# Holding the second half of the first input loads until half of the first mix is done

## What is computed

```
feature: (512, 200, 64) float32      weight: (200, 64, 64) float32
bilinear = einsum('bie,ied->bid', feature, weight)
out      = einsum('bid,bjd->bij', bilinear, feature)      # (512, 200, 200)
```

## Time and profile before

| what | value |
|---|---|
| median of 3 runs | 310.88 us (308.45 to 311.99) |
| the profiled execution | 306.8 us |
| its span, first to last instruction | 305.0 us |
| mean granted TensorE clock | 0.961 |
| TensorE matmuls busy | 243.2 us (80%) |
| VectorE / ScalarE / GpSimd busy | 50% / 43% / 4% |
| DMA, mean over the span | 368 GB/s |

### The profile page before, as it was taken

One profiled execution on the slowest core, in us unless ns is written; L12 is line 12 of the kernel. 1 busy time (PEld: TensorE's weight loads), 2 busy tenths in 40 slices (PEclk: granted clock), 3 DMA queues, 4 the chain that ended last, 5 costly groups with the idle time before them and its releaser, 6 DMA issues.

```text
span 305.0 us, 14640 instructions
## 1 busy us (share of the span) xinstructions
PE 243.2 (80%) x6800; PEld 210.9 (69%) x6800; DVE 152.8 (50%) x180; ACT 130.1 (43%) x181; POOL 12.5 (4%) x23
## 2 busy tenths in 40 slices
PE   6839849999877586999867785898985774998990
PEld 2437749888776476878866675866885674996970
DVE  0153634556755443537644454634765554775621
ACT  2153515445544324245444243542653451665420
POOL 2004800000000000000000000000000000000000
PEclk9996997999999979899999799999999999999997
DMA  7999997999999999968999999986999999599995
GB/s 219 415 417 357 363 410 302 324 376 373 369 360 416 407 419 420 409 280 354 374 366 408 383 411 417 388 355 248 389 371 391 408 387 417 210 402 381 409 408 218
DMA packets 22172, 112.35 MB, mean 368 GB/s; under 512 B 4320, under 2 KB 4320, under 8 KB 21856
## 3 DMA queue, kind: packets, MB, share of 16 engines
q1 hardware_dynamic: 22112, 111.43, 92.6%
HBM read 29.49 MB, written 81.92 MB: 365 GB/s over the span
## 4 chain that ended last, share of the span: by engine, by line
PE 76%; issue 16%; DMA 2%; SPq 2%; DVE 1%; ACT 1%
PE psum L322 50%; PE psum L285 17%; PE psum L339 8%; DMA w_sb<-w_dram 2%; SPq L166 2%; PE psum L305 1%; DVE tile L355 1%; ACT mixed L376 0%; ACT w_sb L390 0%; SPq L178 0%
## 5 line engine op out<-in xcount | busy, mean ns | idle before, releaser
L322 PE MATMUL psum<-x_sb,mixed 64*64 64x200 f32 x3072 | 163.1, 351 | 14.0 <-issue 12.5
L322 PEld LDWEIGHTS psum<-x_sb,mixed 64*64 64x64 f32 x3072 | 133.3, 139 | 27.9 <-issue 17.9
L355 DVE COPY tile<-psum 128x800 f32<-128x800 f32 x100 | 99.2, 992 | 88.6 <-PE psum L322 79.8
L355 ACT COPY tile<-psum 128x800 f32<-128x800 f32 x100 | 82.4, 826 | 70.2 <-PE psum L322 54.0
L285 PE MATMUL psum<-x_sb,w_sb 64*64 64x64 f32 x3072 | 64.4, 221 | 35.1 <-issue 34.2
L285 PEld LDWEIGHTS psum<-x_sb,w_sb 64*64 64x64 f32 x3072 | 61.7, 134 | 40.5 <-issue 37.7
L376 ACT COPY mixed<-psum 64x512 f32<-64x512 f32 x48 | 27.8, 580 | 43.2 <-PE psum L285 42.6
L376 DVE COPY mixed<-psum 64x512 f32<-64x512 f32 x48 | 33.1, 689 | 16.7 <-PE psum L285 15.5
L378 ACT COPY mixed<-psum 128x512 f32<-128x512 f32 x24 | 14.1, 586 | 36.3 <-PE psum L285 36.2
L378 DVE COPY mixed<-psum 128x512 f32<-128x512 f32 x24 | 16.6, 691 | 22.3 <-PE psum L285 22.2
L339 PE MATMUL psum<-x_sb,tails 128*32 128x200 f32 x512 | 25.0, 342 | 0.1
(11 more groups left out here) (5 smaller groups left out, 1.7 us busy)
## 6 DMA issues: line engine op xcount, KB each, us to landing
out_dram<-tile SPq DMA_DIRECT2D x192, 400.0 KB, 5.6
x_sb<-x_dram SPq DMA_DIRECT2D x64, 400.0 KB, 6.9
out_tail_dram<-tile SPq DMA_DIRECT2D x8, 400.0 KB, 4.2
w_sb<-w_dram SPq DMA_DIRECT2D x1, 1152.0 KB, 15.2
w_sb<-w_dram SPq DMA_DIRECT2D x4, 256.0 KB, 7.3
w_sb<-w_dram SPq DMA_DIRECT2D x1, 1024.0 KB, 13.1
```

Of the source, the lines that this page charges most:

```text
L322: last = nc.tensor.matmul(psum[half_rows(pair), n % BANK_PAIRS * 2 + h, a * FIELDS:(a + 1) * FIELDS], mixed[half_rows(h), (CHUNKS * g + c) ...
L355: copy(tile[:, k % SLOTS, engine], psum[:, bank:bank + 2, 0:2 * FIELDS]).then_inc(copied[engine], 1)
```

## The change

SP now waits, behind W pieces 1 to 3, until TensorE has finished two of the four units of the first mix. Then come part 1's first two loads (its piece 0), W piece 4, part 1's other six loads, and W piece 5. The order of these is changed only in that W piece 4 stands behind two of part 1's loads and not behind all eight. No other engine's program changes.

```
@@ -183,10 +183,16 @@
                 load_part0(sp, 0, n)
             for n in range(1, MIX_UNITS):
                 load_w(n)
-            for n in range(X_LOADS):
+
+
+            sp.wait_ge(unit_ready, MIX_UNITS // 2)
+
+            for n in range(X_STRIPS):
                 load_part1(sp, 0, n)
-            for n in range(MIX_UNITS, len(W_CUTS) - 1):
-                load_w(n)
+            load_w(MIX_UNITS)
+            for n in range(X_STRIPS, X_LOADS):
+                load_part1(sp, 0, n)
+            load_w(MIX_UNITS + 1)
```

## The result

The changed kernel takes 310.39 us in the median of 12 runs (307.5 to 313.09), the kernel before 309.99 us in 12 (308.45 to 311.99). The ratio on record is 1.011, interval 1.0068 to 1.0151: slower by about 1%, where the forecast said 1% faster. That ratio is taken over fast runs alone, and the runs listed here don't reproduce it: the means of the 12 and 12 are 310.4 and 310.3 us. Two more timings gave ratios of 1.0068 (1.001 to 1.0126) and 1.0059 (0.9997 to 1.012). Over all timings the mean of 36 runs of the changed kernel is 311.0 us (standard error 0.5), that of 110 runs of before 309.6 us (0.2): 1.4 us slower, give or take 0.5. Timing by timing the means differ by 0.1, 1.4 and 1.7 us. So the change brings no gain, and it costs about 1 us, which is not far outside the noise. A single profile can't show so little at its end: spans of the same code scatter by several us.

What follows compares the result with a forecast made beforehand. TensorE, busy 80% of 305.0 us, loses some 50 us to stalls, read as late instruction pages. Of a 4.4 us lead 2.95 us stay: 306.8 to 303.85 us profiled, 310.88 to 307.9 us median; range 305.0 to 312.5 us.

Steps and rivals of the forecast that it cites:

- What the stalls are: TensorE's stalls without a semaphore: ends of 256-instruction pages where the next page was not there; first one 3.59 us.
- the rival built on it: First mix: the 3.59 us stall is no late page, so it stays; 310.9 us, chance 0.22 for all "stall stays" cases.
- the case that the change does not do what it says: Counted within the rival that the first stall stays: 310.9 us, chance 0.22 together.
- The empty rings: First mix: rings dry from 14.1 us, page asked for at 14.85 us comes at 17.7 us; stall 3.59 to 0.8 us.
- First scores and clock: After the first mix: scores begin at 20.4 us, 2.4 us earlier, and end at 23.4 us with the clock held.
- W of chunk 1: W landed 22.5 us, GpSimd's copies done and chunk 1's mix at 23.8 us, page turn 24.0 us, 4.4 us ahead.
- What is late next: Page behind 24.0 us takes 6.3 us behind loads and stores, ending at 30.3 us; of 4.4 us 2.95 us stay.
- The lead moves along unchanged: Behind the 30.3 us page end, later pages are as slow as before, so the 2.95 us lead stays to the end.
- The slower rival: Lost DMA time fills later dry spells; if the first stall is not shortened, later pages cost 3.3 us: 314.2 us, chance 0.13.

Runs made afterwards that it cites:

- the order alone: The changed kernel without SP's wait, loads in the new order: ratios to the kernel before 1.0133 and 1.0011, mean of 18 runs 309.3 us.
- the wait for four units: The changed kernel with SP waiting for all four units of the first mix, not two: ratio to the kernel before 1.0267, mean 315.2 us.

## Why the prediction was wrong

**What the stalls are** was right: page ends, by the run with more warm-ups. The Trainium skill's rule that fetch is hidden ("Runtime: NRT & Kernel Launch", section "Instruction fetch mechanics") does not hold here; the rival built on it, and the case that the change does not do what it says, fall with the first stall of 1.13 to 1.26 us in three profiles. That this rival's number, 310.9 us, lies next to the measured 310.4 us is luck.

**The empty rings** were right: packet 0.7 us behind the ask (0.5 taken), 18.2 us (17.7). The rings were not dry from 14.1 us, though. The 4.32 MB that had moved by then hold some bytes of part 1; the last packet of the first W pieces ended at 14.7 us before and 14.8 us in the changed kernel, 0.2 us ahead of the ask. So the page met empty rings by a narrow margin.

**First scores and clock** were right: 20.88 us (20.3 and 21.15 us in the other two profiles), taken as 20.0 to 21.0 us, at clock 1.00. In one of the three profiles the clock did fall, at 25.75 us, while TensorE waited for W.

**The step that failed** is "W of chunk 1": landed 22.5 us, chunk 1's mix at 23.8 us, page turn at 24.0 us. Measured in three profiles: landed 24.8 to 25.7 us, mix at 26.1 to 27.1 us, turn at 26.4 to 27.3 us.

W piece 4's packets can be told in the traces by their size, 8192 bytes: in the first profile the last of them ends at 24.85 us, 3.45 us behind the 21.4 us of the sum. Of this 0.3 us are the start of the data (17.2 us, not 16.9), 0.75 us the rate (1.87 MB at 358 GB/s, the mean from there to 24.85 us, and not at 418), and 2.4 us are 0.86 MB of later loads that moved before W was whole, which the sum had left out. The landing was told 0.4 us after the last packet and not 1.1 us, which gives 0.7 us back: 2.7 us in all. Holding those loads back did not bring W sooner, since the rate then fell further.

With rings that are never dry the same sum comes out nearly right, partly by luck: for the order alone it gives 14.1 + 4.5 + 1.1 = 19.7 us, and W landed at 19.7 and 20.65 us, though there too 0.6 MB of later loads moved in front, at 425 GB/s. There W's packets are spread over 3.9 us, in the changed kernel over 5.1 to 5.4 us. So I had taken the rate, and the share of bytes in front of W's last packet, from full rings. The profile of before has lower rates at its start (286 to 326 GB/s from 2.6 to 8 us, 397 and more behind that), which I had not weighed. Why W's packets take longer behind the pause is not settled.

**"What is late next"** was right in mechanism and size: that page took 6.9, 6.0 and 6.0 us in the three profiles (6.3 taken, ends 5.8 and 6.5). It started 2.8 us late on average, and it ended at 33.1 us on average where I had 30.3 us, 2.8 us late as well. So all of the lead that is missing at 33 us (2.95 us counted, 0.15 us left) is W's.

**"The lead moves along unchanged"** can't be held either. The order alone is 2.5 to 2.9 us ahead of before at the turn of 45.56 us, and 0.35 (0.6) us in the end. Delays carry better: the wait for four units is 2.4 us late there and 5.5 us in the end. What evens out leads, and what makes the change 1.4 us slower while it is level at 33 us and only 0.4 us late at the turn of 45.56 us (mean of three 45.95 us), stays open; the single profiles scatter too much behind 50 us.

**The slower rival** had the right side, but its 3.3 us were added up for a first stall that stays. Its last sentence, that it decides where the first stall gives back less than 3.3 us and what W's earlier place brings, is what happened: the stall gave back 2.3 us, and by 33 us that was gone.

## What to carry to other kernels

Where TensorE's stalls have no semaphore, count its instructions between them. Here they stand 256 apart, which makes them page ends, and the pages came late while the DMA rings were full. Draining the rings on purpose to let one page through bought that page and made the loads behind the pause late; compare such a change with the same order of loads and no pause, which here was as good or better. Cost loads behind a pause by rates from a pause of the same kernel, not from full rings, and count the bytes of later loads that move before the one that you wait for is whole.

## What the runs showed of the hardware

A page's packet waited 0.7 to 0.9 us behind the page turn with dry rings in the three profiles of the changed kernel. With the loads or stores running it waited 2.6 to 5.1 us in the first profiles of both kernels up to 48 us. TensorE went on 2.2 to 2.9 us behind the packet in 59 of the 60 page stalls of over 0.7 us that lie before 50 us in the traces (3.8 us in one, of the order alone). With 6.5 MB of stores less in the first group, TensorE was busy 14.3 us of 16 us and not 10.2 us. After 2.4 us without data, the loads of the changed kernel ran at 362 to 393 GB/s up to 24 us, and at 276 to 350 GB/s with six of them also held back; without the pause the order alone ran at 402 to 436 GB/s from 14 to 20 us.
